# Two path blocks of 12 tiles, with the sums shared by three engines and the scaled segments in PSUM

## The reference

```
x1 = x_nodes[src].reshape(-1, N_SEG, EXTENT)        # 16 segments of 32 numbers
x2 = x_edges.reshape(-1, N_SEG, EXTENT)
contrib = path_coeffs[None, :, None] * x1[:, i1, :] * x2[:, i2, :]      # 64 paths
edge_out = jnp.zeros((x2.shape[0], N_SEG, EXTENT), x_nodes.dtype).at[:, i3, :].add(contrib)
out = jnp.zeros((n_nodes, OP_SIZE), x_nodes.dtype).at[dst].add(edge_out.reshape(-1, OP_SIZE))
```

## Time and profile before

| what | us |
|---|---|
| median of 3 timed runs | 278.94 (278.84 to 278.99) |
| the profiled execution | 276.58 |
| its span, first to last instruction | 274.8 |
| TensorE busy | 261.9 |
| VectorE busy | 223.9 |
| ScalarE busy | 169.2 |
| GpSimd busy | 39.7 |

### The profile page before, as it was taken

How to read it: one execution, slowest core, us unless ns; L and a number is a source line. 1 busy time by engine, 2 the same in 40 slices (tenths; PEclk the granted TensorE clock), 3 DMA queues, 4 the chain that set the end, 5 groups by cost and what they waited for, 6 DMA issues and landing times.

```text
span 274.8 us, 5663 instructions
## 1 busy us (share of the span) xinstructions
PE 261.9 (95%) x1631; PEld 184.8 (67%) x1639; DVE 223.9 (81%) x663; ACT 169.2 (62%) x341; POOL 39.7 (14%) x52
## 2 busy tenths in 40 slices
PE   6899999999999899998999999969999999999996
PEld 4566698886444799996778786746666664468633
DVE  5977665199757999999999999999999987655272
ACT  6931351011526999988888888499889829353260
POOL 4000060060005766661000000000000000000000
PEclk9999999999999999999999999989999999999999
DMA  6799990000004665555342000014444429000002
GB/s 193 239 411 408 448 403 21 0 2 1 1 38 122 194 182 146 165 156 155 86 141 83 2 1 1 2 27 146 156 155 156 151 87 347 27 2 2 2 0 76
DMA packets 12593, 33.91 MB, mean 123 GB/s; under 512 B 3346, under 2 KB 3603, under 8 KB 12307
## 3 DMA queue, kind: packets, MB, share of 16 engines
q1 hardware_dynamic: 10482, 26.73, 27.1%
q0 software_dynamic: 2080, 6.82, 8.7%
HBM read 32.50 MB, written 1.05 MB: 122 GB/s over the span
## 4 chain that ended last, share of the span: by engine, by line
PE 83%; DVE 8%; ACT 4%; issue 2%; DMA 1%; DVEq 1%; ACTq 0%; SPq 0%
PE psum L1345 15%; PE psum L1294 15%; PE psum L1248 10%; PE psum L1348 8%; PE psum L1272 5%; PE psum L1277 4%; PE psum L1300 3%; PE psum L1419 3%; PE psum L1445 3%; PE psum L1191 3%; PE psum L1177 2%; DVE big L1039 2%; PE psum L1336 2%; PE psum L1200 1%; PE psum L1457 1%
## 5 line engine op out<-in xcount | busy, mean ns | idle before, releaser
L1294 PE MATMUL psum<-big,dst_oh 128*128 128x512 f32 x108 | 50.6, 593 | 0.2 <-DVE big L1039 0.2
L605 ACT ACTIVATE prod<-edges,coef_b 128x320 f32 (+1 forms) x78 | 43.9, 593 | 11.1 <-PE psum L1348 9.1
L1345 PE MATMUL psum<-prod,ident 128*128 128x128 f32 x160 | 31.8, 293 | 0.8 <-DVE prod L1029 0.7
L1345 PEld LDWEIGHTS psum<-prod,ident 128*128 128x128 f32 x160 | 24.4, 190 | 10.2 <-issue 9.4
L1029 DVE TENSOR_TENSOR prod<-big,prod 128x320 f32<-128x320 f32 (+1 forms) x53 | 30.1, 570 | 0.2 <-DVE big L1000 0.2
L1294 PEld LDWEIGHTS psum<-big,dst_oh 128*128 128x128 f32 x108 | 18.7, 191 | 14.7 <-issue 14.3
L1248 PE MATMUL psum<-edges,big 128*128 128x256 f32 x128 | 28.3, 380 | 0.0
L1039 DVE TENSOR_TENSOR big<-big,prod 128x64 f32 (+2 forms) x80 | 27.6, 345 | 0.4 <-issue 0.2
L605 ACT ACTIVATE xparts<-edges,coef_b 128x320 f32 (+1 forms) x48 | 26.0, 589 | 1.0 <-PE psum L1345 0.8
L1248 PEld LDWEIGHTS psum<-edges,big 128*128 128x128 f32 x128 | 24.1, 190 | 3.5 <-issue 0.3
L470 POOL DMA_INDIRECT big<-xn_rows,big x16 | 17.0, 1064 | 30.5 <-DMA xn_rows<-xn 23.5
(11 more groups left out here) (222 smaller groups left out, 530.0 us busy)
## 6 DMA issues: line engine op xcount, KB each, us to landing
big<-in_w SPq DMA_DIRECT2D x3, 2048.0 KB, 16.2
edges<-in_edge SPq DMA_DIRECT2D x1, 3584.0 KB, 23.9
edges<-in_f SPq DMA_DIRECT2D x7, 512.0 KB, 3.4
edges<-in_edge SPq DMA_DIRECT2D x1, 2560.0 KB, 23.8
edges<-in_edge SPq DMA_DIRECT2D x5, 512.0 KB, 3.6
edges<-in_f SPq DMA_DIRECT2D x1, 2560.0 KB, 10.5
big<-in_f SPq DMA_DIRECT2D x4, 512.0 KB, 3.4
big<-in_gnn_w SPq DMA_DIRECT2D x1, 1024.0 KB, 6.3
```

The source lines that it names most:

```text
L605: nc.scalar.activation(slot(n)[:, 0:BLOCKS[b], :], segment(edges_of(b), single_column(words, p)), ACT.Copy, scale=coef_b[:, p:p + 1]).then ...
L1294: last = mm(bank[2 + h], dst_oh[:, n % DR, h * P:(h + 1) * P], tile_sums(b, t), start=False, stop=False)
L1345: last = mm(path_sums(to), ident[:], product[:, 0:PT].rearrange("p t u -> p (t u)"), start=False, stop=True, skip_group_check=True)
```

## The change

Blocks 1 and 2 get 12 tiles each. In both, TensorE sums four tiles (`KEPT` is 4, so L1348 and the extra PSUM banks are needed in block 0 alone). From path 8 of block 1 and path 5 of block 2 on (`pooled`), GpSimd adds four tiles (`POOLED`, in a new function) and VectorE the last four; before these paths VectorE adds all eight. For a pooled path, `scale` writes no slot but one of two PSUM banks, by turns (`scaled_at`: bank 0 or 1), and waits until the multiply of two paths earlier is done; the multiply reads its second operand from there and writes the slot. There are 13 slots in place of 12. `copy_sums` comes as one piece, at path 8 of block 1 and path 5 of block 2; GpSimd clears the sums of block 2, which ACT did before. The first two paths of block 2 are direct too. The last eight tiles in place of seven are split into bf16 parts, so four tiles are scattered in fp32 at the end. Several buffers move: block 2's edge rows, the sums of block 2, and the weights of the last layer.

```diff
-    BLOCKS = [10, 14, 10]
-    FIRST = [0, 10, 24]
-    KEPT = [8, 6, 4]
+    BLOCKS = [10, 12, 12]
+    FIRST = [0, 10, 22]
+    KEPT = [8, 4, 4]
...
-    SLOTS = 12
-    OWN_SLOTS, XN_SLOTS, PART_SLOTS = 5, 2, 3
+    SLOTS = 13
+    OWN_SLOTS, XN_SLOTS, PART_SLOTS = 5, 2, 4
...
-    DIRECT = [0, 2, 0]
-    SUMS_LEAD = 8
+    DIRECT = [0, 2, 2]
+    SUMS_LEAD = [0, 8, 5]
+    POOLED = 4
...
-    SPLIT = 7
+    SPLIT = 8
...
+        def pooled(n):
+            b, p = divmod(n, NP)
+            return b > 0 and p >= SUMS_LEAD[b]
...
+        def scaled_at(n):
+            if pooled(n):
+                return bank[n % 2][:, 0:BLOCKS[n // NP] * U].rearrange("p (t u) -> p t u", u=U)
+            return slot(n)[:, 0:BLOCKS[n // NP], :]
...
+            pool.wait_ge(mults, NP)
+            nc.gpsimd.memset(rest_sums[2], 0.0).then_inc(cleared[2], 1)
...
+            def add_pooled(n):
+                b, p = divmod(n, NP)
...
+                v = segment(rest_sums[b][:, 0:POOLED, :], out_column(words[b], p))
+                if not pooled(n - 1):
+                    pool.wait_ge(sums, n)
+                if pool_sums_at(n):
+                    pool.wait_ge(pool_sums, pool_sums_at(n))
+                pool.wait_ge(mults, n + 1)
+                nc.gpsimd.tensor_tensor(v, v, slot(n)[:, PT:PT + POOLED, :], ALU.add).then_inc(pool_sums, 1)
...
+                if pooled(n):
+                    if not pooled(n - 1):
+                        act.wait_ge(block_out, banks_before(b))
+                    act.wait_ge(mults, n - 1)
+                elif n >= SLOTS:
...
-                nc.scalar.activation(slot(n)[:, 0:BLOCKS[b], :],
+                nc.scalar.activation(scaled_at(n),
...
-                nc.vector.tensor_tensor(v, segment(xg[:, 0:tiles, :], first_column(words[b], p)), v, ALU.mult).then_inc(mults, 1)
+                if pooled(n):
+                    dve.wait_ge(psums, n + 1 - SLOTS)
...
+                nc.vector.tensor_tensor(v, segment(xg[:, 0:tiles, :], first_column(words[b], p)), scaled_at(n), ALU.mult)\
+                    .then_inc(mults, 1)
...
-                v = segment(rest_sums[b], out_column(words[b], p))
-                nc.vector.tensor_tensor(v, v, slot(n)[:, KEPT[b]:BLOCKS[b], :], ALU.add).then_inc(sums, 1)
+                skip = POOLED if pooled(n) else 0
+                v = segment(rest_sums[b][:, skip:, :], out_column(words[b], p))
+                nc.vector.tensor_tensor(v, v, slot(n)[:, KEPT[b] + skip:BLOCKS[b], :], ALU.add).then_inc(sums, 1)
```

More of the change, by code:

```diff
@@ L152, in slot, with pool_sums_at @@
             return slots[n % SLOTS]
+        def pooled(n):
+            b, p = divmod(n, NP)
+            return b > 0 and p >= SUMS_LEAD[b]
+        def pool_sums_at(n):
+            return sum(pooled(m) for m in range(n))
+        def scaled_at(n):
+            if pooled(n):
+                return bank[n % 2][:, 0:BLOCKS[n // NP] * U].rearrange("p (t u) -> p t u", u=U)
+            return slot(n)[:, 0:BLOCKS[n // NP], :]
         def direct(b, p):
@@ L164, in graph_and_experts @@
         take = carve(big[:, :])
-        x1g = [take([BLOCKS[0], D]), take([BLOCKS[1], D])]
+        late_edges = take([BLOCKS[2], D])
+        x1g = [late_edges[:, 0:BLOCKS[0], :], take([BLOCKS[1], D])]
         late_sums = take([BLOCKS[1] - KEPT[1], D])
@@ L173, in graph_and_experts @@
         path_i = take([NP, 3], I32)[0:1]
-        kept_sums = [sum_room[0][:, 0:KEPT[0], :], x1g[1][:, 0:KEPT[1], :], sum_room[0][:, 0:KEPT[2], :]]
-        rest_sums = [sum_room[0][:, KEPT[0]:, :], sum_room[1], sum_room[0][:, KEPT[2]:, :]]
+        kept_sums = [sum_room[0][:, 0:KEPT[0], :], x1g[1][:, 0:KEPT[1], :], late_edges[:, 0:KEPT[2], :]]
+        rest_sums = [sum_room[0][:, KEPT[0]:, :], sum_room[1], edges[:, 0:BLOCKS[2] - KEPT[2], :]]
         take = carve(x1g[1].rearrange("p t f -> p (t f)"))
@@ L184, in edges_of @@
         def edges_of(b):
-            lo = FIRST[b] if b < NB - 1 else 0
-            return edges[:, lo:lo + BLOCKS[b], :]
+            return edges[:, FIRST[b]:FIRST[b] + BLOCKS[b], :] if b < NB - 1 else late_edges
         take = carve(late)
@@ L215, in graph_and_experts @@
         w_cat = take([KC, G + EX])
-        take = carve(x1g[0].rearrange("p t f -> p (t f)"))
+        take = carve(sum_room[0].rearrange("p t f -> p (t f)"))
         f1_parts = [take([KC // 2, f1.shape[1]])]
-        ctrl_sb = take([KC, ES])
+        f2_parts = [take([2, D])]
+        ctrl_sb = carve(edges[:, BLOCKS[2] - KEPT[2]:BLOCKS[0], :].rearrange("p t f -> p (t f)"))([KC, ES])
         take = carve(edges[:, BLOCKS[0]:LATE, :].rearrange("p t f -> p (t f)"))
         f1_parts.append(take([KC // 2, f1.shape[1]]))
-        f2_lo = take([6, D])
+        f2_parts.append(take([4, D]))
         f2_hi = carve(late)([FC - 6, D])
-        take = carve(big[:, BLOCKS[0] * D:])
+        take = carve(big[:, :])
         xnT2 = take([KC, N])
@@ L319, in f2_sb @@
         def f2_sb(c):
-            return f2_lo[:, c, :] if c < 6 else f2_hi[:, c - 6, :]
+            return f2_parts[0][:, c, :] if c < 2 else f2_parts[1][:, c - 2, :] if c < 6 else f2_hi[:, c - 6, :]
         x_in, idx_in, w_in, w1_in, w3_in, w2_in = (sem(n) for n in
@@ L416, in _ @@
             w = f1.shape[1] // 2
+            sp.wait_ge(scattered, FIRST[1])
             for i in range(2 * KC):
@@ L422, in _ @@
                 sp.wait_ge(mults, NP * (NB - 1) + 44 + 3 * i)
-                sp.dma_start(f2_lo[:, i:i + 2, :], rows(f2)[:, i:i + 2, :]).then_inc(f2_in, 16)
+                sp.dma_start(f2_parts[0] if i == 0 else f2_parts[1][:, i - 2:i, :], rows(f2)[:, i:i + 2, :]).then_inc(f2_in, 16)
             sp.wait_ge(mults, NP * NB)
@@ L494, in _ @@
             gather_rows(2)
+            pool.wait_ge(mults, NP)
+            nc.gpsimd.memset(rest_sums[2], 0.0).then_inc(cleared[2], 1)
+            pool.wait_ge(packed, 3)
+            words = [None, load_words(pool, 0, ROW_PATHS), [None] * ROW_PATHS]
+            def add_pooled(n):
+                b, p = divmod(n, NP)
+                if words[b][p % ROW_PATHS] is None:
+                    words[b][p % ROW_PATHS] = moved(pool, words[b - 1][p % ROW_PATHS], NS ** 6 - 1)
+                v = segment(rest_sums[b][:, 0:POOLED, :], out_column(words[b], p))
[5 more added lines that the diff above has]
+                nc.gpsimd.tensor_tensor(v, v, slot(n)[:, PT:PT + POOLED, :], ALU.add).then_inc(pool_sums, 1)
+            for n in range(NP * NB):
+                if pooled(n):
+                    add_pooled(n)
         @block.scalar
@@ L631, in _ @@
                 b, p = n // NP, n % NP
[L632 to L638, removed]
+                if b and p == SUMS_LEAD[b]:
+                    copy_sums(b - 1, 0, len(sum_banks(b - 1)))
                 for m in range(DR, T - SPLIT):
@@ L643, in _ @@
                     scale(n)
[L644 to L647, removed]
             for m in range(DR, T - SPLIT):
@@ L1017, in multiply @@
                     if direct(b, 0):
-                        dve.wait_ge(edge_in[b], 16)
+                        dve.wait_ge(edge_in[b], 16 if b < NB - 1 else 16 * (BLOCKS[b] // 2))
                 v = slot(n)[:, 0:tiles, :]
@@ L1028, in multiply @@
                 dve.wait_ge(scaled, sum(not direct(*divmod(m, NP)) for m in range(n + 1)))
-                nc.vector.tensor_tensor(v, segment(xg[:, 0:tiles, :], first_column(words[b], p)), v, ALU.mult).then_inc(mults, 1)
+                if pooled(n):
+                    dve.wait_ge(psums, n + 1 - SLOTS)
+                    if pool_sums_at(n + 1 - SLOTS):
+                        dve.wait_ge(pool_sums, pool_sums_at(n + 1 - SLOTS))
+                nc.vector.tensor_tensor(v, segment(xg[:, 0:tiles, :], first_column(words[b], p)), scaled_at(n), ALU.mult)\
+                    .then_inc(mults, 1)
             def add(n):
@@ L1350, in _ @@
                     last.then_inc(psums, 1)
-                    if KEPT[b] > PT and b and p % 2 and p < NP - 1:
+                    if b == 1 and p % 2 and p < NP - 1:
                         mm(bank[4][:, 0:N], zero_b[:], iota_b, start=False, stop=True, skip_group_check=True)
```

15 lines of the change are left out of this document (11 added, 4 removed).

## The result

The changed kernel takes 283.88 us (median of 4 runs, 282.91 to 284.94) beside 278.97 for the kernel before on the same chip: a ratio of 1.0168, 95% interval 1.013 to 1.0205. It is slower by 4.9 us; the forecast was 3.0. The four runs lie in two pairs (282.91 and 282.98, 284.79 and 284.94), so the median stands between them. The profiled execution took 282.91, its span is 281.1.

What follows compares the result with a forecast made beforehand. VectorE was taken to bound the kernel until its last add, then TensorE's tail. VectorE's work and tail -8.9, new loop +10.9, one-hots +1.0: +3.0 us, from 278.94 to 281.9; range 274.5 to 289, the forecast's own 279.5 to 285.

Steps and rivals of the forecast that it cites:

- The new wait: Pooled paths: multiply, handover, scale, handover form a 1.53 us loop for two paths, 0.765 a path; +10.9 us over 115 paths.
- One-hots: ScalarE, between scales: each one-hot puts it 0.05 us over the pace; some 20 in pooled paths, +1.0 us.
- VectorE's work: Blocks 1 and 2: 0.67 us a pooled path, 0.803 before; block 1 43.9 us (-11.7), block 2 44.0 (-0.3).
- rival 1: VectorE stays the bound because handovers cost little more than 0.03 us: pace 0.67, 270.0 us; 14 in 100.
- The blocks: With the loop in place, block 1 should take about 49.8 us and block 2 about 50.1.
- the tail: TensorE at the end: one more fp32 scattered tile and one more split tile, +3.1 us, 16.4 long.
- The sign on VectorE: In pooled paths VectorE should stand idle 0.1 us a path before its multiply, released by ScalarE's scale into PSUM.
- The rule on PSUM sources: VectorE instructions: the skill's table gives a fixed cost of 58 cycles with an SBUF source, 120 with a PSUM one.
- Rival 2: A shorter loop in pooled paths: 1.42 us with handovers of 0.15 and 0.17, pace 0.71, 275.6 us; 11 in 100.
- Rival 3: GpSimd's add and VectorE's add cannot run together: loop up to 1.61 us, 286.5 us, or 289; 18 in 100.
- What costs nothing: TensorE's load and clock, clears moved to GpSimd, copies of sums, gathers and SP's loads were taken to add no time.
- The base: The median lies 2.4 us above the profiled 276.58, so the forecast was counted from 278.94.

Runs made afterwards that it cites:

- run 1: Changed kernel with ScalarE's pooled scales reading a fixed segment, so no register instruction stands between wait and scale: 276.87 us.
- run 2: Changed kernel with both ScalarE's pooled scales and VectorE's pooled multiplies reading fixed segments: 273.97 us.
- run 9: Changed kernel with the pooled waits on the scale and multiply themselves, not on their register instructions: 274.50 us for 279.07 of the kernel before, ratio 0.9827.
- run 5: Changed kernel with pooled scaled segments in SBUF slots instead of PSUM banks, and without GpSimd's adds: 270.45 us.
- run 4: Changed kernel with pooled scaled segments in SBUF slots instead of PSUM banks, GpSimd still adding: 302.46 us.
- run 3: Changed kernel without GpSimd's adds, four tiles of blocks 1 and 2 keeping sums of zero: 282.20 us.
- Run 8: The kernel before, unchanged, measured and profiled once more: 279.99 us, block 0 at 37.86 us.
- run 10: Changed kernel with pooled waits on scale and multiply, and GpSimd's wait for its last add on the add: 272.19 us for 279.07 of the kernel before, ratio 0.9766.

## Why the prediction was right, and where its sizes were off

The direction and the mechanism were right, the size was 1.9 us short. That it came so near is in part luck: one term was 4.0 us too small, others 2.3 too large.

- **The new wait** is what the forecast said, and runs 1, 2 and 9 show it by taking parts out of the loop. Its terms: the multiply 0.554 (forecast 0.56), the scale into PSUM 0.58 (0.61), and the handovers. Turns with no one-hot in them take 1.566 in the mean (72 of them), so the handovers come to 1.566 - 0.554 - 0.583 = 0.43, forecast 0.17 + 0.19 = 0.36. This is the mis-sized term: 0.07 too little for a turn, 4.0 us over 115 paths, of which the shorter scale and multiply give back 1.9. The step that was wrong: the forecast had 0.03 for a handover without register work, and put 0.17 and 0.19 in its place, which cover the register instruction and the 0.05 behind it. The trace has the 0.03 to 0.04 ahead of the register instruction besides, once in each handover, which is the 0.07.
- **One-hots.** Turns with one in them take 1.593 in the mean, 0.027 more; with 21 of them 0.6 us, forecast 1.0. So 4.0 - 1.9 - 0.4 = 1.7 of the 1.9 is found.
- **VectorE's work.** The pace model held. Run 5 has no loop and no GpSimd: 0.676 and 0.679 for 0.67, blocks 1 and 2 at 44.3 and 44.6 for 43.9 and 44.0. Had VectorE stayed the bound, the change would have been worth what was computed; run 5 took 270.45, rival 1's 270.0.
- **The blocks** were to be 49.8 and 50.1 and are 50.6 and 51.3; the tail was to be 16.4 and is 16.3. ScalarE stands idle until a multiply ends, as named. The sign on VectorE was mis-sized: of the loss of 0.12 a path only 0.04 shows as idle time (4.5 us over 115 paths), because an instruction's row ends some 0.08 after the next one starts when nothing is waited for, and gaps so short carry no releaser.
- **The rule on PSUM sources** (Trainium skill, VectorE: DVE Perf Modes, section on the TRN2 errata) would have made the multiply an estimated 0.065 longer with a PSUM operand. It takes 0.554 from PSUM and, in run 5, 0.55 from SBUF: the rows were right to be followed.
- **Rivals 1 and 2** fall with the loop at 1.57, above the 1.48 at which a gain begins. Rival 2's loop of 1.42 needed handovers of 0.15 and 0.17, and they were longer than the forecast's, not shorter.
- **Rival 3** names a mechanism that exists (run 4), at an add of 0.457, but in the changed kernel it is worth 1.0 us (run 3). The multiply from PSUM lets GpSimd's add through, as the rule beside the rival said it would. The two adds disturbed each other little: VectorE's had a mean of 0.296 for 0.284. What the rival has at its end, that GpSimd waits for its own last add, is the next bound behind the loop, at 0.457 + 0.25 = 0.71 (runs 2 and 9).
- **What costs nothing** cost nothing: the granted clock is 1.00 in all three stages, and TensorE is less busy in block 1 than before.
- **The base.** The profile of the kernel before was 2.4 us below its runs' median, and the forecast added that. Run 8 suggests where it lies: block 0 takes 35.5 in that one profile and 36.8 to 37.9 in the other twelve of this study, of kernels with and without the change. So the profiled executions differ by 6.3, and 4.95 without block 0.

ScalarE's handover without its register instruction is 0.035 in runs 1, 2, 9 and 10, as the earlier trace rows have it. VectorE's cannot be read in the same way: it is still some 0.25 in runs 2 and 9, where the loop is no longer the bound and other waits fill it. That stays open, and so does what holds ScalarE and TensorE up in block 0.

## What to carry to other kernels

When a buffer becomes shorter, write down the loop that it closes (use, handover, refill, handover, divided by the buffers) and compare it with the pace of the engine that was the bound; here a change that took 11 us of VectorE's work from one block (run 5) was lost to it. In such a loop look at what the wait hangs on: an instruction with a dynamic address has its register instruction ahead of it, and moving the wait from that onto the instruction itself took the pace from 0.79 to 0.70, while the same move where the producer runs ahead was worth nothing. A buffer in PSUM may be there to keep VectorE's second operand out of SBUF while GpSimd adds: with all of them in SBUF the loop was gone and the kernel 19.6 us slower.

## What was not expected of the hardware

- With all operands in SBUF, VectorE's and GpSimd's instructions hold each other up (run 4): 0.28 became 0.54 and 0.457 became 0.68, which costs 0.24 to 0.25 a path, about half of GpSimd's add, though the two engines' busy times would have fitted side by side.
- GpSimd's two-input add of 128 numbers takes 0.457, and 0.25 passes until its successor, which waits for it, starts. With the wait on the add the shortest such gap is 0.08 (run 10); the 0.21 in the rows there is a wait for VectorE.
- ScalarE writes 384 numbers into PSUM in 0.58, into an SBUF slot in 0.61 (means of 115 and 9 in the changed kernel).
- In block 0 ScalarE stands still for 3.9 to 5.3 us between 93 and 100 us in twelve of thirteen profiles, and the releasers that the view names change from run to run; the thirteenth has none of it, and its block 0 is 1.4 to 2.4 us shorter.
